# Three and four slots instead of two for the weight streams of a fused recurrent and expert layer

## What is computed

```python
u = einsum('ntc,hc->nth', layernorm(x), W_in)             # 1024 -> 2 x 1536
gate, xh = split(u, 2); xh = causal_depthwise_conv(xh)    # 4 taps
g = einsum('nth,gh->ntg', xh, W_gates) + b_gates          # 1536 -> 2 x 1536
forget, inp = split(g, 2)
alpha = exp(-8 * softplus(forget_base) * sigmoid(forget))
h = scan(alpha, sqrt(1 - alpha**2 + 1e-6) * sigmoid(inp) * xh)
x = x + layernorm(einsum('nth,dh->ntd', gelu(gate) * h, W_out))
# second half: all 8 experts on all tokens, weighted by the top 2 of a softmax, and one shared expert
h1, h3 = xt @ w1[e].T + b1, xt @ w3[e].T + b3
y[e] = swiglu(h1 * h3) @ w2[e].T + b2
x = x + layernorm(sum(cw[e] * y[e]) + shared(xt))
```

## Time and profile before

| | |
|---|---|
| runs | 5990.07, 6317.3, 6285.86 us; median 6285.86 |
| profiled execution | 5822.21 us, span of its slowest core (core 2) 5820.7 us |
| spans of the eight cores | 5772.0 to 5820.7 us, granted clock 0.869 to 0.872 |
| busy share of the span | PE 70%, PEld 28%, DVE 42%, ACT 20%, POOL 11% |
| chain that ended last | PE 58%, DVE 14%, DMA 12%, ACT 10%, issue 6% |
| DMA, of the 16 engines' span | 34.3% by the POOL queue, mean 58 GB/s written |

### The profile page before, as it was taken

One profiled execution on the slowest core, in us unless ns is written; L12 is line 12 of the kernel. 1 busy time (PEld: TensorE's weight loads), 2 busy tenths in 40 slices (PEclk: granted clock), 3 DMA queues, 4 the chain that ended last, 5 costly groups with the idle time before them and its releaser, 6 DMA issues.

```text
span 5820.7 us, 52281 instructions; the slowest of 8 cores (5772.0 to 5820.7 us)
## 1 busy us (share of the span) xinstructions
PE 4084.9 (70%) x16304; PEld 1618.8 (28%) x16304; DVE 2467.3 (42%) x4064; ACT 1187.6 (20%) x1715; POOL 629.2 (11%) x1186
## 2 busy tenths in 40 slices
PE   4566565646466465488888888884488888888884
PEld 1222122212122121133333333331133333333331
DVE  2433432432324323545444444545545444445545
ACT  1332231303213031012211111210012211111210
POOL 1010010101111011011111111110011111111110
PEclk8787788769687686699999999997699999999997
DMA  4343343424244242133433333341033433333341
GB/s 63 60 75 60 60 77 54 68 38 73 40 65 63 41 72 42 18 60 51 69 65 62 58 62 53 64 73 43 19 65 51 70 62 63 61 60 58 61 73 40
DMA packets 179676, 336.65 MB, mean 58 GB/s; under 512 B 19424, under 2 KB 39920, under 8 KB 179280
## 3 DMA queue, kind: packets, MB, share of 16 engines
q0 software_dynamic: 175248, 324.92, 34.3%
q1 hardware_dynamic: 4160, 8.39, 0.4%
HBM read 649.41 MB, written 8.39 MB: 113 GB/s over the span
## 4 chain that ended last, share of the span: by engine, by line
PE 58%; DVE 14%; DMA 12%; ACT 10%; issue 6%; DVEq 1%; ACTq 0%; POOL 0%; POOLq 0%
PE pb L163 58%; ACT bufA L815 3%; DMA w2s<-w 3%; DMA wi<-wi_xh 3%; DMA wo<-wout 2%; DMA wi<-wi_gate 2%; DVE sh L467 1%; DVE sa L449 1%; ACT L445 1%; ACT sla L445 1%; DMA wg<-wgates 1%; ACT L501 1%; DMA sxbf<-xin 1%; DVE ssqbf L359 1%; DVE sxnbf L364 1%
## 5 line engine op out<-in xcount | busy, mean ns | idle before, releaser
L163 PE MATMUL pb<-xn,wq 128*128 128x512 bf16 x9216 | 2039.6, 379 | 267.0 <-ACT bufA L815 267.0
L163 PEld LDWEIGHTS pb<-xn,wq 128*128 128x128 bf16 x9216 | 882.1, 98 | 1429.9 <-issue 411.6
L163 PE MATMUL pb<-sxh,wg 128*128 128x512 bf16 x2304 | 649.1, 448 | 341.1 <-ACT ssf L501 202.7
L163 PE MATMUL pb<-a_s,w2s 128*128 128x512 bf16 x2304 | 556.6, 400 | 194.0 <-DVE a_s L870 124.1
L815 ACT ACTIVATE bufA<-pb,c_b1g 128x512 f32<-128x512 f32 x256 | 175.9, 687 | 1741.7 <-PE pb L163 1741.7
L163 PE MATMUL pb<-sxnbf,wi 128*128 128x512 bf16 x1152 | 332.0, 433 | 243.1 <-DMA wi<-wi_xh 105.0
L820 DVE SCALAR_TENSOR_TENSOR bufA<-pb,c_b3g,bufA 128x512 f32<-128x512 f32 x256 | 192.2, 751 | 674.2 <-ACT bufA L815 674.2
L163 PEld LDWEIGHTS pb<-sxh,wg 128*128 128x128 bf16 x2304 | 249.6, 112 | 740.4 <-issue 573.2
L163 PEld LDWEIGHTS pb<-a_s,w2s 128*128 128x128 bf16 x2304 | 226.0, 102 | 516.4 <-issue 297.4
L849 DVE TENSOR_TENSOR bufA<-bufA,bufC 128x512 f32<-128x512 f32 x288 | 199.6, 693 | 241.4 <-ACT bufC L844 241.4
L904 DVE TENSOR_TENSOR racc<-racc,pb 128x512 f32<-128x512 f32 x224 | 154.1, 688 | 347.5 <-PE pb L163 347.5
(11 more groups left out here) (143 smaller groups left out, 2882.9 us busy)
## 6 DMA issues: line engine op xcount, KB each, us to landing
wg<-wgates POOLq DMA_DIRECT2D x192, 384.0 KB, 4.6
wq<-w1g POOLq DMA_DIRECT2D x128, 256.0 KB, 4.6
wq<-w3g POOLq DMA_DIRECT2D x128, 256.0 KB, 5.7
wq<-w1l POOLq DMA_DIRECT2D x128, 256.0 KB, 6.7
wq<-w3l POOLq DMA_DIRECT2D x128, 256.0 KB, 7.5
w2s<-w POOLq DMA_DIRECT2D x128, 256.0 KB, 4.0
wi<-wi_xh POOLq DMA_DIRECT2D x96, 256.0 KB, 3.9
wi<-wi_gate POOLq DMA_DIRECT2D x48, 256.0 KB, 3.8
```

Of the source, the lines that this page charges most:

```text
L163: t.matmul(o, l, r, start=s1, stop=s2),
```

## The change

`WStream` takes the number of its slots from the list it is given, and makes one semaphore for each. `wi`, `wg` and `w2s` get three slots, `wo` four; the four `wq` streams keep two. In wo four loads are asked for ahead of a pass, and each group is followed by the load for the one four further on. The slots cost 2 + 3 + 2 KB more for each partition in the first half and 2 KB in the second.

```diff
-            self.sems = (sem + "0", sem + "1")
+            self.n = len(slots)
+            self.sems = tuple(f"{sem}{j}" for j in range(self.n))
@@ load
-            if i >= 2:
-                assert (i - 2) in self.release, f"{self.tag}: load {i} before release of {i-2}"
-                waits.append(self.release[i - 2])
-            self.ready[i] = g_dma(self.slots[i % 2][:], src_ap, waits=waits,
-                                  sem=self.sems[i % 2], tag=f"{self.tag}{i}")
+            if i >= self.n:
+                assert (i - self.n) in self.release, \
+                    f"{self.tag}: load {i} before release of {i - self.n}"
+                waits.append(self.release[i - self.n])
+            self.ready[i] = g_dma(self.slots[i % self.n][:], src_ap, waits=waits,
+                                  sem=self.sems[i % self.n], tag=f"{self.tag}{i}")
@@ slot and wait: i % 2 becomes i % self.n
@@ streams
-            wi = WStream([asb(f"wi{j}", [128, NC_D, 128], BF16) for j in range(2)], "wi", "wi")
-            wg = WStream([asb(f"wg{j}", [128, NC_H, 128], BF16) for j in range(2)], "wg", "wg")
-            wo = WStream([asb(f"wo{j}", [128, 4, 128], BF16) for j in range(2)], "wo", "wo")
+            wi = WStream([asb(f"wi{j}", [128, NC_D, 128], BF16) for j in range(3)], "wi", "wi")
+            wg = WStream([asb(f"wg{j}", [128, NC_H, 128], BF16) for j in range(3)], "wg", "wg")
+            wo = WStream([asb(f"wo{j}", [128, 4, 128], BF16) for j in range(4)], "wo", "wo")
@@ wo stage
-                    lis = {0: wo.load(d_wo2[pss * NC_H]),
-                           1: wo.load(d_wo2[pss * NC_H + 1])}
+                    lis = {kk: wo.load(d_wo2[pss * NC_H + kk]) for kk in range(4)}
...
-                        if k + 2 < NC_H:
-                            lis[k + 2] = wo.load(d_wo2[pss * NC_H + k + 2])
+                        if k + 4 < NC_H:
+                            lis[k + 4] = wo.load(d_wo2[pss * NC_H + k + 4])
@@ second half
                 w2s = WStream([fsb(f"w2s{j}", [128, E, 128], BF16)
-                               for j in range(2)], "w2s", "w2")
+                               for j in range(3)], "w2s", "w2")
```

More of the change, by code:

```diff
@@ L212, in slot @@
         def slot(self, i):
-            return self.slots[i % 2]
+            return self.slots[i % self.n]
         def wait(self, i):
-            return (self.sems[i % 2], self.ready[i])
+            return (self.sems[i % self.n], self.ready[i])
         def done(self, i):
```

## The result

The changed kernel takes 5489.28 us in the median of ten runs, where the kernel before takes 5831.42 us in the median of its ten: a ratio of 0.942, 95% interval 0.941 to 0.943. Single runs of either kernel are up to 10% longer, with a lower granted clock on the cores of one or both dies wherever the clocks were noted; the three runs of before that were shown ahead of the prediction are 2.9 to 8.6% above the shortest of the ten, and the ratio leaves such runs out.

What follows compares the result with a forecast made beforehand. TensorE bounds the kernel, losing time to waits on two-slot weight loads and the half clock after them. Terms 158 + 97 + 42 + 66 = 363 us turn 5822.21 into 5459, rescaled to 5900; range 5430 to 6010.

Steps and rivals of the forecast that it cites:

- The range: Predicted time of the changed kernel, 5430 to 6010 us, around the named 5900.
- wi, forecast 158: Eight wi stages: groups 2.09 us apart instead of 3.14; light stages 13.2 us less, main 26.2 less.
- The loop: wi stage: 2.43 us to issue plus 3.84 to the next group, 6.27 us shared by three groups instead of two.
- the rival of stretched loads: Loads stretch with more in the air: wi 66, wo 26, wg 15 us less gain; 256 gained; chance 0.21.
- wo, forecast 97: Four wo stages: 24.3 us less each, first pass 11.2 and second 13.1, with groups at 1.4 us.
- wg, forecast 42: Eight wg stages: only each first pair gains, 4.7 us, 38 in all, plus 4; steady pairs gain zero.
- The 4 us added for late loads: wg stages: 4 us added to 38 for the few pairs thrown off by late loads.
- w2s, forecast 66: w2s stages: DMA waits of 63.4 us vanish, plus 3 for shared-expert loads and half clock; bounds 55 and 80.
- The signs that were named: Signs of right, on stage waits, paces and lengths; signs of wrong: wi landing over 4.8, wo groups over 2 us, clock below 0.87.

Runs made afterwards that it cites:

- E7: Changed kernel with each wi load fetching half its block, which the matmuls use twice; 5428.83 us in a single run.
- E6: Changed kernel with four wi slots instead of three; ratio 0.935, profiled 5430.91 us.
- E8: Changed kernel with only the first three wi blocks ever loaded and all wi groups computing with them; profiled span 5429.4 us.
- E3: Kernel before with three slots for wg only, other streams at two; ratio 0.999 (0.995 to 1.004).
- E5: Changed kernel with wg back at two slots; 5517.19 us, ratio 0.947.
- E9: Same kernel as E3, measured again in more rounds; profiled 5796.06 us against 5822.21 before, 0.9955.

## Why the prediction was right, and where it was wrong

**The change in time.** The working was made against the profiled execution, 5822.21 us, and gave 363 us less, 5459 us, a ratio of 0.938. Measured: 5488.08 us, 334 us less, 0.942. The sign, the stages and the mechanism are right.

**The step that failed.** It is the one in which the sum was put on another scale: "The same ratio puts that median at 5894 ... I name 5900." The three runs shown had a median of 6285.86, 1.080 of the profiled execution, and this was taken as the usual time of the kernel. Over ten runs the median before was 5831.42, within 0.2% of the profiled execution. So 5900 as a time is 7.5% above the 5489.28 measured, and beside the real median of before it would even be a slowdown. The profiled execution was the better guide, and nothing in the working needed the other one. The range held the 5489.28 only because its lower end had been drawn out towards that scale.

The terms below are held against core 2, from whose rows they were worked out; the mean of the cores stands behind it.

**wi, forecast 158, measured 128 (mean of the cores 114).** This is the term of the sum that was mis-sized. The loop had the right form, but its landing time was held at 3.8 us "since two loads already in the air 2.4 us apart both landed in time". That reading was right for two slots: the gate blocks of before, over all cores, landed after 3.75 us when nothing else of the core was in the air at their issue and after 3.76 when one load was. It did not carry over to three. There the median was 4.6 us for the gate blocks on core 2 and 4.8 over all cores, and the loop with these, (2.43 + 4.6) / 3 = 2.34 and (2.43 + 4.8) / 3 = 2.41 us a group, is what the gate stages show: main stages less light ones, over their 48 groups, (271.7 - 161.7) / 48 = 2.29 on core 2 and (274.3 - 158.7) / 48 = 2.41 as a mean of the cores, not 2.09. E7 shows that the growth goes with the bytes, as the rival of stretched loads had it; that rival's own price, 2.64 a group, was too high. E6 and E8 show what was left: 87 us above the floor, 58 of which the fourth slot takes.

The prediction set beside this a rule of the Trainium skill ("DMA: Bandwidth & Descriptors", the anatomy section), 2 us plus bytes over 436 GB/s. By the trace of before, loads issued with no other of their core in the air landed after 2.9, 3.8 and 4.5 us for 128, 256 and 384 KB written (wo, wi and wg, medians over all cores): a fixed part of about 2 us agrees; the rate behind it is 0.52 MB more read in 1.7 us, 308 GB/s, so here the measured landings decide and not the page's rate.

**wo, forecast 97, measured 105 (mean 108).** The end of the first pass was forecast to go to VectorE's last product, and it did. The second pass did about as 1.4 us a group had it: the row at 1078.89 has 21 matmuls in 7.22 us, 1.4 a group with half of it at the lower clock, and after it the groups are 1.1 to 1.5 apart. The second pass gained 14 us a stage (13.1 forecast) and the first 12 (11.2): it ends 1.2 us after the product (1072.34 + 1.02), where 2.0 was allowed, since the last group ran at the upper clock.

**wg, forecast 42, measured 34 (mean 31).** The step that mattered, that the largest DMA wait of the list is covered and only the first pair gains, is confirmed by the stages of E3 and by E5 and E9. In the stage shown the first pair itself gave the 4.7 us forecast (15.39 to 10.71). Over all cores the second pair starts 6.0 us earlier in light and 7.1 in main tiles, but the chain takes part of it back: from its odd block on only 3.5 and 4.9 us are left, 34 us for the eight stages. The steady pairs repeat as before. The 4 us added for late loads did not show. The wait for `ssf` rose to 330 us, more than the 300 forecast, and that cost nothing: the pairs are as long, so what their matmuls no longer need became waiting.

**w2s, forecast 66, measured 78 (mean 68).** The reason was right: the waits are gone and the stage is one piece of matmuls. The size was 12 short on core 2. The waits for `w` and `sw` loads were 63.4 + 6.1 us, and the same matmuls are busy for 548.9 us instead of 556.6, 7.7 less; the forecast allowed 3 for both.

**Sum and cores.** On core 2 the stages measured give 345 us where the terms add up to 363, and the rest is 11 us longer, which no step had: 334. As a mean of the cores they give 322, less 6. Before, the cores lay 48.7 us apart, and in each pair of neighbours (0 and 1, 2 and 3, and so on) one was 34 to 37 us behind the other. The largest part of this was w2s: its stages took 632 to 640 us on the four slower cores and 611 to 620 on the others. With three slots for w2s alone (E4) they take 555 to 558 on all, and neighbours lie 11 to 22 us apart. After the full change all cores lie within 14.5 us. So part of the gain is one of the metric, which takes the slowest core: a stage that is not paced by its loads is alike on all cores. That the neighbours' loads collide is a guess that no run tested.

**The signs that were named.** wi waits down from 172 to 70 us, not under 40; groups 2.3 to 2.4 apart, not 2.1; wo 38 us (40 named); w2s 30.6 (31 named); wg 3.9 us less a stage (5 named); clock over the run 0.876 to 0.881, not lower. The landing of wi at 5.0 is over the 4.8 that was named as what would make the forecast wrong; it cost most of what is missing in wi, 30 us on core 2: 120 groups at 2.29 and not 2.09 are 24.

## What to carry to other kernels

Treat a stream of loads as a loop: pace of a group = (time from its start to the next issue + landing) / slots, not under the group's own time nor the queues' time for the bytes; and expect landing to grow with each further load that is let into the air (here by 1.1 and 0.6 us, where the transfer itself, at 159 GB/s written, is 1.65). Take from the wait list only those waits behind which no longer one stands in the same period. And make a forecast of a time on the scale of the execution whose rows it was worked out from; three runs that lie 3 to 8.5% above it are a reason for a wide range, not for another centre.

## What the runs showed of the hardware

- Landing of a 256 KB load (0.52 MB read as float32) in the wi stages, median of `wi_xh` on the slowest core: 3.9 us with two slots, 5.0 with three, 5.6 with four; 3.2 with three slots and half the bytes. For the gate blocks over all cores: 3.8, 4.8, 5.1 and 3.0. In 15 us of the gate stage the queues are 78% busy at 106 GB/s, where a stretch of before reached 94% and 159 GB/s, so loads stretch well short of that.
- A wait inside a stage can cost more than itself: the wo stages of core 2 waited 84.9 us for loads, of which 71 went, and became 105 us shorter, 46 of it in the busy time of the same matmuls (153.3 to 106.8), since the granted clock rose from 0.67 to 0.87 in the stage.
- A wait that stands ahead of a longer chain costs nothing: the stand ahead of the odd wg block went from 4.3 to 7.7 us and the pairs repeat every 21.10 and 22.06 us, as they did (20.97 and 22.13).
